# Scans of a state space model: 128 channels on the partitions, or 4 states of 32 channels

## The reference

```python
x_dbl = jnp.einsum('bkdl,kcd->bkcl', xs, x_proj_weight)      # 12 rows for dt, 16 of B, 16 of C
delta = jax.nn.softplus(dts + dt_projs_bias[None, :, :, None])
A = -jnp.exp(A_logs)                                         # (4, 384, 16)
def step(hstate, inp):
    dl, ul, bl, cl = inp
    hstate = jnp.exp(dl[..., None] * A) * hstate + (dl * ul)[..., None] * bl[:, :, None, :]
    y = jnp.einsum('bkdn,bkn->bkd', hstate, cl)
    return (hstate, y)
_, ys = jax.lax.scan(step, h0, (delta_t, u_t, B_t, C_t))     # over the 4096 pixels
ys = ys + Ds * u
y = ys[:, 0] + ys[:, 2, :, ::-1]                             # reversed directions are folded back
```

## Time and profile before

| what | us |
| --- | --- |
| median of 3 runs | 27879.47 |
| lowest and highest | 27868.37, 27930.98 |
| the profiled execution | 27921.66 |
| its span (first to last instruction) | 27919.9 |

### The profile page before, as it was taken

How to read it: one execution, slowest core, us unless ns; L and a number is a source line. 1 busy time by engine, 2 the same in 40 slices (tenths; PEclk the granted TensorE clock), 3 DMA queues, 4 the chain that set the end, 5 groups by cost and what they waited for, 6 DMA issues and landing times. The chain is left out here.

```text
span 27919.9 us, 261599 instructions
## 1 busy us (share of the span) xinstructions
PE 24874.1 (89%) x70946; PEld 10612.0 (38%) x70946; DVE 25291.2 (91%) x22482; ACT 17866.2 (64%) x30091; POOL 23560.1 (84%) x10168
## 2 busy tenths in 40 slices
PE   8788988998888899889888888988889988888888
PEld 3333443443443344344344434434334433333332
DVE  8899999999999999999999999999851189999996
ACT  2477777777777777777777777777423266666662
POOL 1599999999999999999999999999502189999994
PEclk9999999999999999999999999999999999999999
DMA  5533333333333343333333333333543277777778
GB/s 202 193 140 148 150 140 145 147 142 141 151 143 142 145 152 138 145 150 144 140 149 149 138 147 149 141 143 150 178 133 109 79 232 230 229 229 230 230 230 293
DMA packets 1194275, 4583.10 MB, mean 164 GB/s; under 512 B 254368, under 2 KB 292272, under 8 KB 827472
## 3 DMA queue, kind: packets, MB, share of 16 engines
q1 hardware_dynamic: 1093568, 4217.15, 42.5%
q10 hardware_dynamic: 99248, 349.22, 3.4%
HBM read 3907.28 MB, written 658.64 MB: 164 GB/s over the span
## 5 line engine op out<-in xcount | busy, mean ns | idle before, releaser
L1049 DVE TENSOR_TENSOR_SCAN s_h<-s_dA,s_state,s_dbu 128x512 f32<-128x512 f32 x12236 | 14960.7, 1269 | 59.2 <-ACT s_dA L884 50.7
L971 POOL TENSOR_TENSOR s_dbu<-s_du,s_b_sb 128x1536 f32<-128x1536 f32 (+1 forms) x4610 | 14188.6, 3084 | 430.9 <-DMA s_b_sb<-rows 428.7
L884 ACT ACTIVATE s_dA<-s_delta,s_negA 128x512 f32<-128x512 f32 x12288 | 8289.9, 685 | 5515.3 <-DVE s_h L1049 5501.6
L711 PE MATMUL s_y_ps<-s_hc,s_ident 128*128 128x512 f32 x17920 | 8785.2, 602 | 1.5 <-DVE s_hc L1059 1.5
L983 POOL TENSOR_TENSOR s_hc_pool<-s_h,s_c_sb 128x512 f32<-128x512 f32 (+1 forms) x4864 | 7843.8, 1617 | 575.4 <-DVE s_h L1049 514.6
L721 PE MATMUL s_y_ps<-s_hc_pool,s_ident 128*128 128x512 f32 x12800 | 6379.7, 600 | 105.2 <-ACT s_yo L846 105.2
L1059 DVE TENSOR_TENSOR s_hc<-s_h,s_c_ps 128x1024 f32<-128x1024 f32 (+1 forms) x5632 | 5526.0, 981 | 169.5 <-issue 140.9
L711 PEld LDWEIGHTS s_y_ps<-s_hc,s_ident 128*128 128x128 f32 x17920 | 3491.1, 195 | 2162.5 <-issue 1932.4
L1049 DVE TENSOR_TENSOR_SCAN s_h<-s_dA_sb,s_state,s_dA 128x512 f32<-128x512 f32 x3060 | 3816.0, 1266 | 295.1 <-PE s_dA L672 290.8
L701 PE MATMUL s_c_ps<-s_bc,s_sel 96*128 96x512 bf16 x6400 | 2369.0, 390 | 1455.2 <-DVE s_hc L1059 1441.2
L721 PEld LDWEIGHTS s_y_ps<-s_hc_pool,s_ident 128*128 128x128 f32 x12800 | 2379.7, 193 | 2786.9 <-issue 2532.9
(11 more groups left out here) (175 smaller groups left out, 17734.1 us busy)
## 6 DMA issues: line engine op xcount, KB each, us to landing
s_b_sb<-rows SPq DMA_DIRECT2D x1794, 1024.0 KB, 6.8
s_c_sb<-rows SPq DMA_DIRECT2D x1216, 1024.0 KB, 5.2
s_u<-U SPq DMA_DIRECT2D x257, 768.0 KB
Y<-s_yo ACTq DMA_DIRECT2D x256, 768.0 KB, 3.8
s_prev<-Y SPq DMA_DIRECT2D x128, 768.0 KB, 4.4
s_u<-U SPq DMA_DIRECT2D x193, 256.0 KB
U<-f_row SPq DMA_DIRECT2D x24, 2048.0 KB, 17.3
U<-f_col SPq DMA_DIRECT2D x24, 2048.0 KB, 7.1
```

The costliest lines, as they stand in the source:

```text
L711: last = pe.matmul(y_ps[:, t, :], ident[:, :], hc[:, s % 2, j, :], start=begins(g, s), stop=nd > 1 and s == NS - 1)
L884: act.activation(place, delta[g % 2][:, t, :], ACT.Exp, scale=negA[g % 2][:, a:a + 1]).then_inc(dA_ready, 1)
L971: pool.tensor_tensor(dbu[:, i % AHEAD, :, :], a, b, ALU.mult).then_inc(dbu_ready, 1)
L1049: dve.tensor_tensor_scan(h[:, s % (2 * GROUP), j, :], decay, given, initial, ALU.mult, ALU.add).then_inc(scanned, 1)
```

## The change

The first layer's scans get a function of their own, `packed_scans`; `scan_phase` stays for the second layer. The units, and the way in which directions are folded, are the same. What differs:

- A tile holds 4 states x 32 channels on its 128 partitions, by 512 steps. A unit has again 48 tiles: 12 steps (m) of 4 tiles (i); a step is 4 states (group m // 3) of 128 channels (block m % 3), tile i has channels 32i to 32i+31 of the block.
- All of du * B is made with time on the partitions: duT times B into `scaled`, for a group of 4 states at a time (1536 elements per state). Of the 16 states of a unit ACT makes 9, with 4 instructions each, DVE 5 and POOL 2, with one TENSOR_TENSOR each, whose second input is the column of `rowsT` repeated. PE turns every tile into `x_ps` (a ring of 4 banks).
- The decay needs delta of 32 channels on four groups of partitions. delta is stored to DRAM (`store_delta`) and read back spread by four DMAs per block (`spread_delta`). ACT writes the decays to SBUF, in a ring of 8.
- C is read from DRAM, each of 4 rows broadcast to 32 partitions. The products by C, all of them, are made by POOL, one instruction of 2048 elements per step, into `hc` (ring of 2). In front of it POOL copies the last column of h, 128x4, in the seven units of eight that have a next one. h is a ring of 3 steps.
- The sum over states adds the four groups of partitions too: `fold` has 128 rows and 32 columns, and product i writes partitions 32i to 32i+31 of `y_ps`.
- The bf16 split of the rows of B and C (`rest`, lines 634 and 635) and the broadcasts of C by PE are gone.

The diff, cut to its core (PE, POOL, DVE and the parts of ACT and SP that feed them):

```diff
+    NG, NJ, NI, R = 4, ND0, 4, 4
+    STEPS, QB = NG * NJ, T // 128
+    TILES = STEPS * NI
+    units = B * K0 * NCHUNK
+    DECAYS, INPUTS, H_RING, REP = 8, 4, 3, 4
+    BY_ACT = ((0, 1), (0, 1), (0, 1, 3), (0, 1))
+    BY_DVE = ((2, 3), (2,), (2,), (2,))
+    BY_POOL = ((), (3,), (), (3,))
+    on_pe = dict(xproj=0, rows=1, dt=(2, 3, 4), turn_du=(7, 8, 8))
+    on_act = dict(take=0, rows=1, dt=(2, 3, 4), soft=5, turn_du=(7, 8, 8), evacuate=(0, 1, 2), store=3)
+    on_pool = dict(du=6)
+    SCALE_ACT = {0: (1, 0), 1: (1, 1), 3: (2, 0), 4: (2, 1), 6: (3, 0), 7: (3, 1), 9: (4, 0), 10: (4, 1)}
+    SCALE_DVE = {1: 1, 4: 2, 7: 3, 10: 4}
+    SCALE_POOL = {0: 1, 6: 3}
...
+        delta_rep = sb("delta_rep", [128, REP, NI, T])
+        duT, rowsT = sb("duT", [128, QB, NJ * NI, 32]), [sb(f"rowsT{q}", [128, QB, N_STATE]) for q in range(2)]
+        scaled = sb("scaled", [128, 2, QB, NJ * NI, R, 32])
+        c_sb = [sb(f"c_sb{q}", [128, NG, T]) for q in range(2)]
+        dA = sb("dA", [128, DECAYS, T])
+        h, hc = sb("h", [128, H_RING, NI, T]), sb("hc", [128, 2, NI, T])
+        x_ps = pb("x_ps", [128, INPUTS, T])
...
+            def spread_c(g):
+                eng.wait_ge(xd_ready, g + 1)
+                wait(eng, c_in[g % 2], g // 2 * 16 * R)
+                eng.dma_start(rows_dram[g % 2, 0:N_STATE, :], xd[N_STATE:ROWS_BC, :]).then_inc(rows_stored, 16)
+                eng.wait_ge(rows_stored, 16 * (g + 1))
+                wait(eng, hc_ready, (g - 1) * STEPS)
+                for r in range(R):
+                    rows = rows_dram[g % 2, r:N_STATE:R, :]
+                    eng.dma_start(c_sb[g % 2][32 * r:32 * r + 32, :, :],
+                                  rows.unsqueeze(0).broadcast_to([32, NG, T])).then_inc(c_in[g % 2], 16)
...
+            def store_delta(g):
+                eng.wait_ge(delta_ready, g + 1)
+                for x in range(max(NJ * (g - 2), 0), NJ * (g - 1)):
+                    eng.wait_ge(rep_in[x % REP], 16 * R * (x // REP + 1))
+                eng.dma_start(delta_dram[g % 2], delta[:, :, :]).then_inc(delta_stored, 16)
+                eng.wait_ge(delta_stored, 16 * (g + 1))
+            def spread_delta(g, j):
+                x = NJ * g + j
+                if x >= REP:
+                    before, last = divmod(x - REP, NJ)
+                    eng.wait_ge(dA_ready, before * TILES + (STEPS - NJ + last + 1) * NI)
+                for r in range(R):
+                    eng.dma_start(delta_rep[32 * r:32 * r + 32, x % REP, :, :],
+                                  delta_dram[g % 2, :, j, :].rearrange("(i c) t -> c i t", c=32)).then_inc(rep_in[x % REP], 16)
...
+            def turn_input(n, i):
+                tile, x = n * NI + i, n // NJ
+                if n % NJ == 0 and i == 0:
+                    pe.wait_ge(scaled_act, QB * scaled_to(BY_ACT, x + 1))
+                    pe.wait_ge(scaled_dve, scaled_to(BY_DVE, x + 1))
+                    wait(pe, scaled_pool, scaled_to(BY_POOL, x + 1))
+                wait(pe, scanned, tile - INPUTS + 1)
+                for b in range(QB):
+                    last = pe.transpose(x_ps[:, tile % INPUTS, b * 128:(b + 1) * 128],
+                                        scaled[:, x % 2, b, n % NJ * NI + i, :, :].rearrange("p r c -> p (r c)"), ident[:, :])
+                last.then_inc(input_turned, 1)
...
+            def state_sum(n):
+                g, m = divmod(n, STEPS)
+                if m < NJ:
+                    direct(g, m)
+                pe.wait_ge(hc_ready, n + 1)
+                for i in range(NI):
+                    last = pe.matmul(y_ps[32 * i:32 * i + 32, m % NJ, :], fold[:, :], hc[:, n % 2, i, :],
+                                     start=m < NJ and not opens(g) and not folds(g), stop=m >= STEPS - NJ)
+                last.then_inc(summed, 1)
...
+            def scale(x, part):
+                g = x // NG
+                if part == 0:
+                    act.wait_ge(rows_taken, g + 1)
+                    act.wait_ge(du_taken, (g + 1) * NJ)
+                    wait(act, input_turned, (x - 1) * NJ * NI)
+                for b in range(part * QB // 2, (part + 1) * QB // 2):
+                    for r in BY_ACT[x % NG]:
+                        s = x % NG * R + r
+                        act.activation(scaled[:, x % 2, b, :, r, :], duT[:, b, :, :], ACT.Copy,
+                                       scale=rowsT[g % 2][:, b, s:s + 1]).then_inc(scaled_act, 1)
+            def decay(n, i):
+                g, m = divmod(n, STEPS)
+                tile, x = n * NI + i, NJ * g + m % NJ
+                if m < NJ and i == 0:
+                    act.wait_ge(rep_in[x % REP], 16 * R * (x // REP + 1))
+                wait(act, scanned, tile - DECAYS + 1)
+                a = m * NI + i
+                act.activation(dA[:, tile % DECAYS, :], delta_rep[:, x % REP, i, :], ACT.Exp,
+                               scale=negA[:, direction(g), a:a + 1]).then_inc(dA_ready, 1)
...
+            def take_du(g):
+                pool.wait_ge(delta_ready, g + 1)
+                pool.wait_ge(loaded[g % 2], 16 * (g // 2 + 1))
+                wait(pool, du_turned, g * NJ)
+                pool.tensor_tensor(du[:, :, :], delta[:, :, :], u[g % 2][:, :, :], ALU.mult).then_inc(du_ready, 1)
+            def scale(x):
+                g = x // NG
+                pool.wait_ge(rows_taken, g + 1)
+                pool.wait_ge(du_taken, (g + 1) * NJ)
+                wait(pool, input_turned, (x - 1) * NJ * NI)
+                for r in BY_POOL[x % NG]:
+                    s = x % NG * R + r
+                    pool.tensor_tensor(scaled_slot(x, r), duT[:, :, :, :],
+                                       rowsT[g % 2][:, :, s:s + 1].unsqueeze(3).broadcast_to([128, QB, NJ * NI, 32]),
+                                       ALU.mult).then_inc(scaled_pool, 1)
+            def times_c(n):
+                g, m = divmod(n, STEPS)
+                pool.wait_ge(scanned, (n + 1) * NI)
+                if goes_on(g):
+                    pool.tensor_copy(state[:, m * NI:(m + 1) * NI], h[:, n % H_RING, :, T - 1]).then_inc(state_saved, 1)
+                if m == 0:
+                    pool.wait_ge(c_in[g % 2], 16 * R * (g // 2 + 1))
+                wait(pool, summed, n - 1)
+                c = c_sb[g % 2][:, m // NJ:m // NJ + 1, :].broadcast_to([128, NI, T])
+                pool.tensor_tensor(hc[:, n % 2, :, :], h[:, n % H_RING, :, :], c, ALU.mult).then_inc(hc_ready, 1)
+            take_du(0)
+            for g in range(units):
+                for m in range(STEPS):
+                    n = g * STEPS + m
+                    if n:
+                        times_c(n - 1)
+                    if m in SCALE_POOL:
+                        scale(g * NG + SCALE_POOL[m])
+                    if m == on_pool["du"] and g + 1 < units:
+                        take_du(g + 1)
+            times_c(units * STEPS - 1)
...
+            def scale(x):
+                g = x // NG
+                dve.wait_ge(rows_taken, g + 1)
+                dve.wait_ge(du_taken, (g + 1) * NJ)
+                wait(dve, input_turned, (x - 1) * NJ * NI)
+                for r in BY_DVE[x % NG]:
+                    s = x % NG * R + r
+                    dve.tensor_tensor(scaled_slot(x, r), duT[:, :, :, :],
+                                      rowsT[g % 2][:, :, s:s + 1].unsqueeze(3).broadcast_to([128, QB, NJ * NI, 32]),
+                                      ALU.mult).then_inc(scaled_dve, 1)
+            def scan(n, i):
+                g, m = divmod(n, STEPS)
+                tile = n * NI + i
+                if i == 0:
+                    wait(dve, hc_ready, n - H_RING + 1)
+                    wait(dve, state_saved, saves_to(n - H_RING + 1) if n >= H_RING else 0)
+                dve.wait_ge(dA_ready, tile + 1)
+                dve.wait_ge(input_turned, tile + 1)
+                a = m * NI + i
+                initial = state[:, a:a + 1] if continues(g) else 0.0
+                dve.tensor_tensor_scan(h[:, n % H_RING, i, :], dA[:, tile % DECAYS, :], x_ps[:, tile % INPUTS, :],
+                                       initial, ALU.mult, ALU.add).then_inc(scanned, 1)
+            scale(0)
+            for g in range(units):
+                for m in range(STEPS):
+                    for i in range(NI):
+                        scan(g * STEPS + m, i)
+                        if i == 1 and m in SCALE_DVE and (SCALE_DVE[m] < NG or g + 1 < units):
+                            scale(g * NG + SCALE_DVE[m])
...
-    scan_phase(nc, "s0", (B, K0, ND0, 1, R0), U0, Y0, rows0, arg["a_xproj"], arg["a_dt"], arg["a_small"],
-               arg["a_D"], arg["keep"], arg["ident"], arg["select"])
+    packed_scans(nc, U0, Y0, rows0, scratch("delta0", (2, 128, ND0, T)), arg["a_xproj"], arg["a_dt"], arg["a_bias"],
+                 arg["a_logs"], arg["a_D"], arg["ident"], arg["fold"])
```

292 lines of the change are left out of this document (288 added, 4 removed).

## The result

The changed kernel takes 29102.66 us (median of 4 runs, 29090.64 to 29108.65) against 27878.91 us for the kernel before on the same chip: a ratio of 1.0435, 95% interval [1.0416, 1.0453]. It is slower, as forecast, and inside the range, but by 1224 us where the forecast had 690.

What follows compares the result with a forecast made beforehand. DVE was taken to set the pace: 65.0 us of work plus 7.4 and 3.9 of port waits made 76.3 us per unit against 73.65, over 256 units +678, with +10 and -42: 28570 us, range 27,900 to 29,700.

Steps and rivals of the forecast that it cites:

- The sign: Whole kernel: slower, chance 0.81, because DVE's two-SBUF-input multiplies and POOL's instructions hold the memory port in turn.
- The floor: First layer's scans: POOL's work and DVE's five multiplies can't overlap, so at least 74.0 us per unit, above 73.65.
- DVE's own time, 65.0: DVE per unit: 56.6 us of scans plus five multiplies of 1.68 us, against 71.6 now.
- POOL's own time, 65.6: POOL per unit: 53.8 us of products by C, 10.2 of 1536-element products, 1.6 of copies.
- The waits at the port, 4 x 1.85 + 3.9 = 11.3: DVE's multiplies wait 1.85 us for POOL in each of four steps, and step 10's second multiply 3.9 more.
- Waits for others, nothing: DVE in the scans: no idle time in the 76.3 us sum; today's 2.0 us only in the upper bound, 80.
- PE, 51 to 62 us busy: PE per unit: transposes 21.1 us, narrow sums about 10 to 21.2, the rest at most 19.3; some 14 us of cover.
- ACT, 64: ACT per unit: 31.0 us of decays, 20.7 of scalings, at most 12.6 of other work; 12 below DVE.
- Rival 3: PE's 32-column products run one at a time: PE needs 82 us, 86 with waits, 31,050 us in all; chance 0.03.
- rival 4: PE's clock falls to 1.2 GHz in the scans, PE doubles to 102 us per unit, 35,150 us; chance 0.02.
- DMA: Delta's store and spread through DRAM cost nothing per unit, only 10 us once at the start.
- Rival 1: POOL's products don't hold the port, or only partly: 68.5 us per unit, 26,560 us, faster; chance 0.13.

Runs made afterwards that it cites:

- the fastest kernel: Changed kernel with B's rows in PSUM, input ring of 3, ACT's products earlier, PE's preparation and a second-tile turning before the sum: 26469.87 us, 0.949 of before.
- the pairs: B's factors for DVE from SBUF against PSUM: with ring of 3, 81.61 against 74.77 us per unit; in the fastest kernel, 79.82 against 68.03.
- the last run: The fastest kernel with DVE's five multiplies taking B's factors from the SBUF copy again instead of PSUM: 29509.36 us, 1.0588 of the kernel before.

## Why the prediction was right in sign and short in size

**The sign** came from the port, and that was right, in mechanism and place. The floor was put at 65.6 + 8.4 = 74.0 us; by the fastest kernel POOL's work is 16515/256 = 64.5 and the five multiplies 5 x 1.73 = 8.7, so 73.2, of which each start-to-end overlap takes a little. So the floor as measured lies 0.4 below the 73.65 of the kernel before, where the prediction had it 0.35 above: by the floor alone the sign was too close to call, and what made the kernel slower is the 5.1 us by which its 78.28 stands above it. The port's share is shown by the pairs: it costs 6.8 us per unit with the old order and 11.8 with the new one, each more than the 4.6 that the change lost. No run has the changed kernel's four places and a free port at once, so its time without the port's waits is not shown.

**DVE's own time, 65.0:** right. The kernels whose multiplies read PSUM have DVE busy 64.7 to 65.6 us per unit.

**POOL's own time, 65.6:** right in sum with two errors in it. The product h by C takes 4.54 us (4.48 said), and the multiply duT x B 2.76, where I had 3.40 from a product whose second input isn't repeated; the copy 0.18 (0.15 said).

**The waits at the port, 4 x 1.85 + 3.9 = 11.3:** too high. They are 5 x 3.21 - 5 x 1.75 = 7.3 us. By step the multiply's mean over all units is 2.35 us in step 1, 4.38 in step 4, 2.16 in step 7 and 3.57 in step 10 (two of them), so waits of 0.6, 2.6, 0.4 and 3.6. Two assumptions failed. I let DVE come upon POOL at a random point; but POOL's product begins when the step's fourth scan is done, and so the multiply, behind the next step's first scans, meets it at nearly the same point each time. And I had the second multiply of step 10 find a POOL instruction waiting (3.9 us); the timeline above shows that there is none, because POOL's next product waits for scans behind the multiplies. From 4000 to 16000 us the first of the two takes 5.35 us on average and the second 1.77.

**Waits for others, nothing:** this is the step that failed. DVE idles 6.0 us per unit. In the sum I gave it none ("waits of one are seldom cover for the other" was applied to the port alone), and in the range only today's 2.0. By DVE's waits, PE takes about 5.0 of the 6.0: 1.2 at step 3's second tile, 0.8 at step 6's, 1.7 at step 9's. The other 0.9 is for POOL, at step 9's first tile. And the wait for PE at step 9 is handed on from POOL too (timeline, DVE and PE):

```profile
9065.47 2.45 DVE L873 TENSOR_TENSOR_SCAN p_h<-p_dA,p_state,p_x_ps 128x512 f32<-128x512 f32 x2 [1.83 <-PE p_x_ps L592]
...
9062.38 1.94 PE L616 MATMUL p_y_ps<-p_hc,p_fold 128*32 128x512 f32 x8 [1.80 <-POOL p_hc L828]
9064.25 1.97 PE L592 MATMUL p_x_ps<-p_ident,p_scaled 128*128 128x128 f32 x8
```

In front of that tile PE had a sum to make that waited for POOL's product, 1.9 us per unit, in 255 of 256 units. POOL was late with it after the two more products of step 6. So 65.0 + 7.3 + 6.0 = 78.3, where the prediction had 65.0 + 11.3 = 76.3: two errors of 4.0 and 6.0 in opposite directions, and the net 2.0 (unrounded 1.98) x 256 = 507 us of the 533 that are missing. That the sum came as near as it did is partly luck: it had the waits at the port too high and left the others out.

**PE, 51 to 62 us busy; ACT, 64:** 57.5 and 58.2, both right or better. What was wrong is the conclusion "some 14 us of cover". PE has 20 us free in each unit and is late nevertheless, since it works a fixed order, and in its steps 2 and 8 a sum stands in front of the tile that DVE wants for steps 3 and 9. Busy time says whether an engine can keep up, not whether it is on time. Running PE's preparation first took the idle time from 9.1 to 3.9 us in the kernel with the port free and ACT's products early; in the changed kernel it took nothing off.

**Rival 3, the narrow products one at a time:** false. The eight records of a step's four products in the timeline of PE take 1.06 us at the full clock:

```profile
9051.77 1.06 PE L616 MATMUL p_y_ps<-p_hc,p_fold 128*32 128x512 f32 x8
```

That lies under the pairs' 1.77 of the earlier trace rows and near the 0.86 that I gave for four at a time.

**The clock, rival 4:** did not decide, and yet I was wrong about it. I foretold over 0.9; it is 0.81, so 39% of the time at the lower of the two levels, 1.2 GHz. PE ahead of one such fall, in it, and behind it (stretches of 4 us; columns as above):

```profile
9048.00:9052.00 4.00, 2.89 (x24) 1.85 (x24) 3.97 (x4) 3.99 (x7) 4.00 (x2) 1.00 0.49 199
9052.00:9056.00 4.00, 1.78 (x15) 0.78 (x8) 4.00 (x4) 4.00 (x8) 4.00 (x2) 0.98 0.92 210
9056.00:9060.00 4.00, 2.85 (x14) 2.45 (x13) 4.00 (x4) 3.08 (x6) 4.00 (x3) 0.50 0.31 58
9060.00:9064.00 4.00, 2.20 (x11) 0.38 (x9) 2.72 (x3) 1.96 (x4) 4.00 (x3) 0.50 0.20 63
9064.00:9068.00 4.00, 3.31 (x22) 2.83 (x19) 2.45 (x2) 0.60 (x1) 4.00 (x3) 0.74 1.01 199
9068.00:9072.00 4.00, 4.00 (x36) 2.67 (x38) 3.46 (x3) 3.97 (x8) 4.00 (x3) 1.00 0.00 0
```

PE was busy 2.89 and 1.78 us of the 4 before, with transposes and narrow sums alone, and got half the clock. My argument from the earlier trace rows rested on a stretch that held plain products as well. The rule that I had set aside (the Trainium skill, "TensorE: Matmul & The Clock Gate", Part 4: transposes don't engage the full clock) is not borne out as it stands either: from 9062 to 9072 us PE again did nothing but transposes and narrow sums, and the clock rose to 1.00. And the fastest kernel, with the same instructions on PE, had 0.92. Whether the idle time or the kind of work lets the clock fall, no run here separates. What it cost is open too: 2.7 us per unit of DVE's waits for PE fall in half-clocked time, and the run with more plain products added work together with clock. Rival 4's 35,150 us did not come, as PE is not the bound at 57.5 us busy.

**ACT:** its decays are not late in the changed kernel (0.8 us in 12,000); in ten of the twelve other kernels of the table they are, by 1.0 to 8.6 us per unit, most where ACT makes DVE's products too.

**DMA:** right. Delta is stored in 3.2 us and spread in 4.7 us (medians of the page), and no wait on DVE is put down to it.

**Rival 1 and its 68.5 us** is of interest for what it described: with the port not held it would have been 65.0 + 2.0 + 1.5. The fastest kernel, which frees the port by another way, stands at 68.03; but that confirms nothing, since it needed three edits of the order besides, and the free port alone gave 74.77 (with a ring of 3).

## What to carry to other kernels

Before a product is moved to VectorE beside a busy GpSimd, look where its two tensor inputs lie. With both in SBUF the multiplies here took turns with GpSimd by whole instructions, even with 2 elements; with one in PSUM they ran free. That one operand was worth 11.8 us of 80 per unit in the best order of work, and 6.8 in the first. And when a bound is taken away, price the next one by the order of work on the other engines and by who waits for what in it, not by their busy time: PE at 77% busy cost 5.6 us per unit, which an edit of its order gave back where ACT's decays had been late behind it, and not in the changed kernel, where they were on time.

## What the runs showed of the hardware that was not expected

- The engine that waits at the port is not always the next to get it, as I had taken from the earlier trace rows. In the last run a multiply issued in the middle of a POOL instruction lets that one and the following one pass (timeline, DVE and POOL):

```profile
15913.39 2.75 POOL L822 TENSOR_TENSOR p_scaled<-p_duT,p_rowsT 128x1536 f32<-128x1536 f32 x1
15914.32 6.83 DVE L866 TENSOR_TENSOR p_scaled<-p_duT,p_rowsT 128x1536 f32<-128x1536 f32 x1
...
15916.11 3.42 POOL L812 TENSOR_TENSOR p_du<-p_delta,p_u 128x1536 f32<-128x1536 f32 x1
15919.48 1.71 POOL L831 COPY p_state<-p_h 128x4 f32<-128x4 f32 x1
```

  The multiply waited 5.1 us through both; then POOL's copy of 4 elements per partition, 0.18 us alone, waited 1.5. The longest of the 2-element multiplies, 6.10 us, was caught in the same way. What decides who is next stays open.
- A POOL multiply of 1536 elements takes 2.76 us with B's factor repeated over a run of elements, and 3.45 us with two full tensors, where DVE doesn't hold it up.
- Four fp32 products into four different quarters of the partitions, 512 columns each, take 1.06 us together at the full granted clock, and 1.94 at half.
- A place less in a ring of four PSUM banks between PE and DVE cost 3.3 us per unit: DVE's idle time went from 6.0 to 8.3, and the multiplies' mean from 3.21 to 3.36.
